# Causal attention at the length of 2,048: small diagonal maxima of several heads share a PSUM bank, are masked by TensorE, and go ahead of the scores

## The reference

```python
q, k = _rope(split_heads(n @ Wq.T)), _rope(split_heads(n @ Wk.T)); v = split_heads(n @ Wv.T)   # n = layernorm(x)
scores = jnp.einsum('bhqd,bhkd->bhqk', q, k) / math.sqrt(dk)
scores = jnp.where(causal[None, None], scores, -jnp.inf)
attn = jax.nn.softmax(scores, axis=-1)
ctx = jnp.einsum('bhqk,bhkd->bhqd', attn, v)
x = x + ctx.transpose(0, 2, 1, 3).reshape(B, S, D) @ Wo.T
x = x + (layernorm(x) @ base_w.T + base_b + 2.0 * lora_of_top_2_experts(layernorm(x)))
```

## Time and profile before

| | |
|---|---|
| median of 3 runs | 1680.56 us (1676.03 to 1681.06) |
| the profiled execution | 1674.16 us, its span 1672.4 us |
| TensorE matmul busy | 1610.6 us (96%) |
| VectorE busy | 1163.7 us (70%) |
| ScalarE busy | 761.8 us (46%) |
| GpSimd busy | 885.6 us (53%) |
| mean granted clock of TensorE | 0.985 |

### The profile page before, as it was taken

The page is one execution under the profiler, slowest core; times in us unless marked ns, Lnnn a source line. Parts: engine busy times, 40 slices in busy tenths (PEclk is TensorE's granted clock), DMA queues, the critical chain, the costliest instruction groups (busy, mean ns, idle before and its releaser), DMA issues. The chain is left out here.

```text
span 1672.4 us, 26163 instructions
## 1 busy us (share of the span) xinstructions
PE 1610.6 (96%) x9440; PEld 985.0 (59%) x9440; DVE 1163.7 (70%) x2667; ACT 761.8 (46%) x1539; POOL 885.6 (53%) x559
## 2 busy tenths in 40 slices
PE   5999999899999999999999999999999987999999
PEld 4888888554455555455445445545545535777776
DVE  5666665778777777777777777777777765665664
ACT  3222222144555556556556556555566563222321
POOL 1333234346767667667667677667667793112111
PEclk9999999679999999999999999999999999999999
DMA  5555784651134125116107107106103003222321
GB/s 189 195 195 178 227 279 163 184 121 33 27 79 100 27 51 128 27 29 144 27 20 159 27 8 170 27 8 152 32 22 108 7 33 102 76 76 76 102 100 51
DMA packets 112327, 157.04 MB, mean 94 GB/s; under 512 B 11600, under 2 KB 44880, under 8 KB 112208
## 3 DMA queue, kind: packets, MB, share of 16 engines
q1 hardware_dynamic: 102368, 136.10, 29.6%
q10 hardware_dynamic: 9840, 19.40, 3.3%
HBM read 96.23 MB, written 58.72 MB: 93 GB/s over the span
## 5 line engine op out<-in xcount | busy, mean ns | idle before, releaser
L836 ACT ACTIVATE a_probs<-a_st 128x512 f32<-128x512 f32 (+2 forms) x1244 | 576.6, 538 | 435.6 <-PE a_st L754 429.2
L710 POOL TENSOR_TENSOR a_pair<-a_probs 128x1024 f32<-128x1024 f32 (+2 forms) x320 | 618.7, 1954 | 208.1 <-ACT a_probs L836 200.8
L856 DVE TENSOR_REDUCE a_part<-a_mx 128x1 f32<-128x512 f32 x768 | 504.3, 683 | 169.6 <-PE a_mx L741 167.2
L860 DVE CUSTOM_DVE_ANT_0 a_mx<-a_mx,a_mask 128x384 f32<-128x384 f32 (+3 forms) x512 | 248.8, 496 | 87.9 <-PE a_mx L741 86.5
L741 PE MATMUL a_mx<-a_k_stack,a_q_stack 96*128 96x512 f32 (+3 forms) x768 | 284.1, 376 | 5.4 <-DVE a_part L860 1.9
L754 PE MATMUL a_st<-a_q_stack,a_k_stack 98*128 98x512 f32 (+3 forms) x732 | 277.4, 394 | 0.1
L754 PEld LDWEIGHTS a_st<-a_q_stack,a_k_stack 98*128 98x128 f32 x732 | 137.6, 189 | 161.8 <-issue 84.8
L248 POOL TENSOR_TENSOR p_rot<-p_mul 128x1024 f32<-128x1024 f32 x32 | 89.9, 2812 | 201.6 <-DVE p_mul L479 201.5
L741 PEld LDWEIGHTS a_mx<-a_k_stack,a_q_stack 96*128 96x128 f32 x768 | 146.1, 190 | 53.2 <-DVE a_part L856 20.2
L741 PE MATMUL a_mx<-a_k_first,a_q_stack 96*128 96x512 f32 (+3 forms) x384 | 161.2, 436 | 7.3 <-DVE a_part L856 2.3
L754 PE MATMUL a_st<-a_q_stack,a_k_first 98*128 98x512 f32 (+3 forms) x384 | 155.6, 415 | 0.0
(11 more groups left out here) (167 smaller groups left out, 2007.9 us busy)
## 6 DMA issues: line engine op xcount, KB each, us to landing
a_q_stack<-qk_scratch SPq DMA_DIRECT2D x72, 256.0 KB, 5.1
a_k_stack<-qk_scratch SPq DMA_DIRECT2D x72, 256.0 KB, 8.1
qk_scratch<-p_rot_hi SPq DMA_DIRECT2D x32, 512.0 KB, 3.1
qk_scratch<-p_rot_lo SPq DMA_DIRECT2D x32, 512.0 KB, 3.9
v_scratch<-p_v_st SPq DMA_DIRECT2D x32, 256.0 KB, 6.7
ctx_scratch<-a_ctx_st SPq DMA_DIRECT2D x32, 256.0 KB, 2.4
f_ctx<-ctx_scratch SPq DMA_DIRECT2D x8, 1024.0 KB, 9.2
f_x<-in_x SPq DMA_DIRECT2D x8, 1024.0 KB, 8.1
```

The source lines that it names most:

```text
L710: pool.tensor_tensor(pair[:, p % 2, h:h + 2, q0:TT], probs[:, s % RING, h:h + 2, q0:TT], probs[:, (s + 1) % RING, h:h + 2, q0:TT], ALU.add ...
L836: act.activation(probs[:, s % RING, h, q0:TT], score_bank(g, HG * s + h)[:, q0:TT], ACT.Exp, scale=SCORE_SCALE).then_inc(exp_done, 1)
L856: dve.tensor_reduce(found, mx_ps[k % MX_BANKS][:, :], AX.X, ALU.max).then_inc(max_done, 1)
L860: dve.tensor_tensor_reduce(out=scores, in0=scores, in1=mask[:, TT - (qi + 1) * P:TT], scale=1.0, scalar=3.0 * MASKED, op0=ALU.add, op1=ALU ...
```

## The change

The items of a unit's diagonal chunk are grouped: for qi = 0 all four heads share one bank (4 x 128 columns), for qi = 1 two heads do (2 x 256), for qi = 2 and 3 each head still has its own. So a group has 140 items instead of 160. For qi = 0 and 1 the mask is no longer added by VectorE: a last matmul of an identity (as weights) with the mask's 128 columns, repeated for each head, adds it to the last 128 columns of each head in PSUM, and VectorE takes the maxima of all heads by one TENSOR_REDUCE. For qi = 2 and 3 VectorE masks as before. In each half the item now stands ahead of the score of the same turn. The masked value becomes -2^126. The identity and the mask are rounded to fp32r copies by two VectorE copies at the end of `project`, for which TensorE waits once at the start of `attend`; to make room, `project`'s identity lies in the tile `early.cin`. All counts that depend on NITEM follow: HEAD_START from 85 to 75, BEFORE_FIRST from 48 to 38, the plan of items a pair, and the banks k % 3 of a group's last items against the next group's first.

```diff
-MASKED = -1e38
+MASKED = -2.0 ** 126
-ITEMS = [(t, qi, h, c) for t in range(QT) for qi in range(SUB) for h in range(HG) for c in range(t + 1)]
+HEADS_OF_ITEM = (4, 2, 1, 1)
+MASKED_BY_PE = (True, True, False, False)
+ITEMS = [(t, qi, h, c) for t in range(QT) for qi in range(SUB) for h in range(HG) for c in range(t + 1)
+         if c < t or (h + 1) % HEADS_OF_ITEM[qi] == 0]
...
+def heads_of_item(t, qi, h, c):
+
+    n = HEADS_OF_ITEM[qi] if c == t else 1
+    return list(range(h + 1 - n, h + 1)), TT if c < t else (qi + 1) * P
...
-        ident = sb("p_ident", [P, P])
+        ident = early.cin[:, 0, 0:P]
...
+            dve.wait_ge(first.mask_done, 1)
+            dve.tensor_copy(first.ident_r[:, :], ident[:, :]).then_inc(first.mask_rounded, 1)
+            dve.tensor_copy(first.later_r[:, :], first.mask[:, TT - P:TT]).then_inc(first.mask_rounded, 1)
...
-                mm = pe.matmul(mx_ps[k % MX_BANKS][:, 0:width], queries[t][0:96, h, qi * P:(qi + 1) * P],
-                               keys[par][c][0:96, h, 0:width], start=True, stop=True)
+                bank = mx_ps[k % MX_BANKS][:, 0:len(heads) * width].rearrange("p (h n) -> p h n", n=width)
+                masked_here = c == t and MASKED_BY_PE[qi]
+                for i, head in enumerate(heads):
+                    mm = pe.matmul(bank[:, i, :], queries[t][0:96, head, qi * P:(qi + 1) * P], keys[par][c][0:96, head, 0:width],
+                                   start=(i == 0), stop=not masked_here and i == len(heads) - 1)
+                if masked_here:
+                    later = first.later_r[:, :].unsqueeze(1).to_broadcast([P, len(heads), P])
+                    mm = pe.matmul(bank[:, :, width - P:width], first.ident_r[:, :], later, start=False, stop=True)
...
                         for i in range(max(HG, len(due))):
+                            if i < len(due):
+                                n, k = due[i]
+                                item(g + n, (par + n) % 2, next_use if n else use, k)
                             if i < HG and s < NSTEP:
                                 scores(g, par, s, i)
                             elif i < HG and not last:
                                 scores(g + 1, 1 - par, s - NSTEP, i)
-                            if i < len(due):
-                                n, k = due[i]
-                                item(g + n, (par + n) % 2, next_use if n else use, k)
...
+            pe.wait_ge(first.mask_rounded, 2)
...
-                found = part[:, h * SUB + qi, c:c + 1]
-                if c < t:
+                heads, width = heads_of_item(t, qi, h, c)
+                found = part_of[:, heads[0]:h + 1, qi, c]
+                bank = mx_ps[k % MX_BANKS][:, 0:len(heads) * width]
+                if c < t or MASKED_BY_PE[qi]:
                     dve.wait_ge(item_done, NITEM * g + k + 1)
-                    dve.tensor_reduce(found, mx_ps[k % MX_BANKS][:, :], AX.X, ALU.max).then_inc(max_done, 1)
+                    dve.tensor_reduce(found, bank.rearrange("p (h n) -> p h n", n=width), AX.X, ALU.max).then_inc(max_done, 1)
```

More of the change, by code:

```diff
@@ L157, in __init__ @@
         self.mask = sb("a_mask", [P, TT])
+        self.ident_r, self.later_r = sb("a_ident_r", [P, P], F32R), sb("a_later_r", [P, P], F32R)
         self.part = sb("a_part", [P, HG * SUB, QT])
@@ L162, in __init__ @@
         self.key_ones = sem("a_key_ones")
-        self.zeroed, self.mask_done = sem("a_zeroed"), sem("a_mask_done")
+        self.zeroed, self.mask_done, self.mask_rounded = sem("a_zeroed"), sem("a_mask_done"), sem("a_mask_rounded")
         self.rot_stored = [sem("p_rot_stored0"), sem("p_rot_stored1")]
@@ L171, in wait_stored, with project @@
             eng.wait_ge(self.v_stored[u], 64 * TILES // 2 + START)
-def project(nc, x, wq_t, wk_t, wv_t, rope, qk_scr, v_scr, shared, first):
+def project(nc, x, wq_t, wk_t, wv_t, rope, qk_scr, v_scr, shared, first, early):
     x_v = x.rearrange("(t s p) d -> t p s d", p=P, s=SUB)
@@ L543, in attend @@
         mask, part = first.mask, first.part
+        part_of = part[:, :, :].rearrange("p (h q) c -> p h q c", q=SUB)
         max_both = sb("a_max_both", [P, 2, HG * SUB])
@@ L732, in item @@
                 t, qi, h, c = ITEMS[k]
-                width = TT if c < t else (qi + 1) * P
+                heads, width = heads_of_item(t, qi, h, c)
                 if k == 0 and use is not None:
@@ L852, in item_max @@
                 t, qi, h, c = ITEMS[k]
-                found = part[:, h * SUB + qi, c:c + 1]
-                if c < t:
+                heads, width = heads_of_item(t, qi, h, c)
+                found = part_of[:, heads[0]:h + 1, qi, c]
+                bank = mx_ps[k % MX_BANKS][:, 0:len(heads) * width]
+                if c < t or MASKED_BY_PE[qi]:
                     dve.wait_ge(item_done, NITEM * g + k + 1)
-                    dve.tensor_reduce(found, mx_ps[k % MX_BANKS][:, :], AX.X, ALU.max).then_inc(max_done, 1)
+                    dve.tensor_reduce(found, bank.rearrange("p (h n) -> p h n", n=width), AX.X, ALU.max).then_inc(max_done, 1)
                 else:
                     wait_alone(dve, item_done, NITEM * g + k + 1, dve_passed)
-                    scores = mx_ps[k % MX_BANKS][:, 0:(qi + 1) * P]
-                    dve.tensor_tensor_reduce(out=scores, in0=scores, in1=mask[:, TT - (qi + 1) * P:TT], scale=1.0,
+                    dve.tensor_tensor_reduce(out=bank, in0=bank, in1=mask[:, TT - width:TT], scale=1.0,
                                              scalar=3.0 * MASKED, op0=ALU.add, op1=ALU.max,
@@ L1429, in layer @@
         early = Early(nc, ctx, shared, ctx_scr, wo_t, x, first)
-        project(nc, x, wq_t, wk_t, wv_t, rope, qk_scr, v_scr, shared, first)
+        project(nc, x, wq_t, wk_t, wv_t, rope, qk_scr, v_scr, shared, first, early)
         early.place()
```

## The result

| | before | after |
|---|---|---|
| median | 1678.3 us (1674.02 to 1681.06, 4 runs) | 1656.22 us (1653.99 to 1658.38, 4 runs) |
| profiled span | 1672.4 us | 1652.8 us |
| TensorE matmul busy | 1610.6 us | 1607.6 us (97%) |
| VectorE busy | 1163.7 us | 1142.6 us (69%) |
| ScalarE busy | 761.8 us | 764.2 us (46%) |

The ratio is 0.9881, 95% interval [0.9859, 0.9902]: 1.2% faster, where 0.9% was forecast. The medians differ by 22.1 us, the profiled spans by 19.6 us; 15.0 us were forecast.

A forecast was written before the change was run, and what follows sets the result against it. TensorE's in-order matmul stream was taken as the bound, its waits for VectorE counting in full. Six groups -10.8, last group -0.7 and first group -3.5 make -15.0 us: 1665.6 us from a median of 1680.56, range 1650 to 1682.

The forecast's parts named there:

- The masks: Mask matmuls added on TensorE for a group's four units, not covered by other work: +1.90 us a group.
- rival 2: A wash, 1677 to 1680 us: half the five-item waits stay, or mask matmuls cost double; chance 0.19.
- Narrow matmuls in a row: Four 128-wide products of different heads in succession: taken as 0, bounds -0.2 and +0.3 us a unit.
- The wrap: From one group's items to the next, bank 0 is reused at once; with 140 items the wait goes: -1.08 us.
- Five-item halves: TensorE's waits for VectorE in halves with five items go: -3.9 us a group, with +0.8 left over.
- What the order costs ScalarE: Scores start 0.33 us later in a half and wait for exponentials: +0.8 us a group, some eight halves.
- Rival 1: Masks paid, waits kept: five-item waits return as waits on ScalarE; +11 us, 1691 us; chance of slower 0.13.
- After units: After a unit's end the fourth item still waits for VectorE but was due earlier: -0.3 us a group.
- The sum of a group: All terms of one whole group together: -1.8 us, and -10.8 us for six groups.
- First group and before: Ramp, items before the first score, wrap and ordinary pairs of the first group together: -3.5 us.
- rival 3: Half-clock stretch changes with denser TensorE work: 1655 or 1675 us; larger gain by clock or waits all gone, 0.13.
- Last group: Items end in its first half; masks 0.48, waits 2.5 falling to 1.2, scores 0.1: -0.7 us.

The follow-up runs named there:

- experiment 10: Changed kernel, items ahead only in halves with five or more, only quarter 0 shared and masked by TensorE (148 items), banks numbered on through groups: 0.9794, 1641.25 us.
- experiment 3: Kernel before, with the items' banks numbered on through all groups instead of starting anew in each: 0.997, 1670.05 us.
- experiment 1: Kernel before with items ahead of scores and nothing else (160 items a group, VectorE masks all): 0.9894, 1657.42 us.
- Experiment 2: Changed kernel with scores ahead of items again, so grouping and masks alone: 0.9873, 1655.03 us.
- Experiments 6 and 7: Changed kernel, items ahead of scores only in halves with at least four, or at least five, items: 0.9829, 1646.4 us, and 0.9817, 1643.54 us.
- experiment 4: Changed kernel with each mask matmul issued twice: 0.9962, 1667.15 us.

## Why the prediction was right, point by point

**The total.** 15.0 us were forecast, 19.6 are the difference of the spans. Its parts were mostly right in kind, but several errors cancel, as the points below show, and that the total came so near is in part luck. The medians differ by 22.1 us because two of the four executions of the kernel before (1680.56 and 1681.06) lie near the top of its range: beside the experiments the same kernel had medians of 1673.0 to 1674.3 us.

**The masks: right.** +1.90 a group was forecast and 1.8 measured from both sides. The doubled price of mask matmuls, one of the two ways of rival 2 to a wash, did not occur.

**Narrow matmuls in a row: taken at nothing, and not nothing.** The prediction held that a 128-wide item costs the same 0.11 us between wide scores as behind another. In PE's timeline of the kernel before it doesn't:

```profile
591.85 0.40 PE L754 MATMUL a_st<-a_q_stack,a_k_stack 98*128 98x512 f32 x1
592.09 0.23 PE L741 MATMUL a_mx<-a_k_stack,a_q_stack 96*128 96x128 f32 x1
592.15 0.45 PE L754 MATMUL a_st<-a_q_stack,a_k_stack 98*128 98x512 f32 x1
```

From score to score it is 0.30 us, so the item adds 0.06. In a row they start 0.11 us apart, and the wide mask behind them takes 0.287 up to the next score instead of 0.235. My estimate from these rows is 0.1 to 0.2 us a unit, 0.5 to 0.8 a group: inside the bounds of the prediction (up to 0.3 a unit), but missing from its sum.

**The wrap: the mechanism right, shown by three kernels.** 160 and 148 items have the gap, whatever the order; 140 items or running banks don't. Its worth depends on what stands behind: 1.2 us in experiment 10, but about 0.7 in experiment 3, because there the third item inherits part of the wait. The forecast took the full 1.08.

**Five-item halves: right in kind, incomplete in cause.** 3.9 us of waits were to go with 0.8 left over, and about 0.8 of item waits are left. But I had given this gain to both parts as one and never asked what either does by itself. Experiments 1 and 2 answer: either removes most of these waits alone. That the items stand ahead of the scores, to which the prediction gave half the credit, was not needed for it.

**What the order costs ScalarE: the mis-sized term.** It was forecast at +0.8 and read at 1.7 a group. The forecast counted some eight halves with three items or fewer; `plan_items` with 140 items gives 19. Experiments 6 and 7, which take the order back where it isn't needed, win 1.25 and 1.5. With this loss in it, the order is worth 127.2 - 128.05 = -0.85 us a group on the grouped kernel: in the whole groups it hurts. Rival 1 named this mechanism, but it stayed far from the size at which it decides. One of the prediction's signs of being wrong, waits on exponentials in place of waits on maxima, is met in part: in the changed kernel they are the larger of the two, 1.7 us against 0.8.

**After units: better than forecast, and by the other part.** About 0.1 is left of 1.16, where 0.85 was expected. The forecast gave the gain to the order; but the order alone leaves both waits (experiment 1), so it is the grouping that removed them. That is 0.75 more, and the ScalarE term took 0.9 back: two errors that cancel.

**The sum of a group.** It gained 2.2 in all instead of 1.8 (13.3 instead of 10.8 for six). The terms as measured give less than that: 1.8 for masks, some 0.6 for narrow matmuls, -1.08, -3.1, -1.05 and +1.7 make -1.1. The rest lies in the waits that stood there before. I summed over one whole group (621.1 to 751.2 us before, 612.0 to 740.0 after) how much later than their pitch (0.235, 0.18, 0.12 and 0.06 us for 512, 384, 256 and 128 columns) the starts behind scores and items come: 15.7 us before and 11.7 after. With the masks' own 1.9 that gives -2.1, the measured gain. Some 7.4 us of either sum are, by my estimate, the edges of the 40 halves (0.10 at the start of each and 0.085 ahead of its values), so 8.3 us rather than 6.2 were lost before. The same sum gives -2.15 for the order alone (13.55) and -3.2 for the grouping alone (10.65).

**First group and before: right in sign, half in size.** Forecast -3.5, measured -7.0 (-5.6 and -1.4, of which 0.5 lie before the first item). The working had the ramp at -3.3 by the order and +2.0 by larger items. Experiment 2, with the grouping and the old order, has the old length (with 3.4 us more at half clock), so the grouping's terms roughly cancel; the order gives 4.4 by itself and 5.8 on the grouped kernel. The half-clock stretch was 10.3 us shorter (44.4 to 34.1), as rival 3 would have it. But one profile of each can't show that the change did it: executions of one kernel differ as much. From the mean granted clocks of the four executions of the changed kernel (0.982 to 0.988) the time at half clock is some 60 to 40 us in all (my estimate: the span times twice what the clock lacks to 1.00), with spans of 1656.6 to 1652.3, and in the 44 executions of the kernel before beside the experiments it is some 50 to 74 us. A straight line through those 44 has the span grow by 0.42 us for each us more at half clock; through the four it is 0.24. At these prices 10.3 us are worth 2.4 to 4.3 us (an estimate), about what the first group gained beyond the forecast. The order alone gains 4.4 us with the stretch at its old 44.4. In the other kernels it was 34.1, 37.5, 41.0 or 44.4, or 17.1 twice with 3.4 between them (experiment 4), with no rule that I can show.

**Last group:** +0.2 instead of -0.7. The grouping alone gives -0.6 and the order alone +1.1. All three have 3.4 us at half clock in this group, the kernel before none; between the two grouped kernels, with the same clock, the order costs 0.8, which the prediction had at +0.1. **Indicators:** the period (128.05 for 128.3), the wrap, 96 masks and the counts of 864 and 256 instructions came as written; "item loads waiting under 2 us" was the wrong thing to look at, and the half-clock stretch moved by 10.3 us, just over the 10 that the prediction named as a sign of being wrong.

## What to carry to other kernels

When an engine's in-order queue is the bound and another engine frees its buffers, a gain may be claimable by either of two edits; try each alone, since their gains need not add and the second may only bring its cost (here the order, which loses 0.85 us a group when applied everywhere and gains 0.65 when applied only to halves with five items). Check the number of uses of a rotating buffer against the number of buffers where a loop starts anew: a remainder of one makes the first use of the new round wait for the use just before it (1.26 us here). Read waits of an in-order queue from one start to the next, since an idle load queue may lie under running matmuls.

## What the runs showed of the hardware

- Four 128-wide matmuls of different weights in a row start 0.11 us apart or a little more, about as far as one 256-wide (0.12); a single one between two 512-wide ones adds 0.06.
- Executions of one kernel differ in their time at half clock, and their spans with it: the mean granted clock was 0.978 to 0.985 in 44 executions of the kernel before, with spans of 1681 to 1669 us.
- An identity matmul that adds to PSUM with gaps of 128 columns between runs of 128 costs 0.12 us for 256 columns, the same as without gaps.
- On VectorE a reduction of 512 columns to 2 or to 4 outputs takes as long as to one. The groups by form in the changed kernel, 413.85 to 541.9 us (count | busy us, mean ns | idle before, releaser):

```profile
L879 DVE TENSOR_REDUCE a_part<-a_mx 128x1 f32<-128x512 f32 x96 | 61.6, 679 | 16.9 <-PE a_mx L758 16.8
...
L879 DVE TENSOR_REDUCE a_part<-a_mx 128x2 f32<-128x512 f32 x8 | 5.4, 684 | 3.0 <-PE a_mx L762 3.0
...
L879 DVE TENSOR_REDUCE a_part<-a_mx 128x4 f32<-128x512 f32 x4 | 2.8, 693 | 1.3 <-PE a_mx L762 1.2
```
